# Sparse attention on one core: the weights of two key tiles added by a DMA ahead of one denominator product

## What is computed

```python
logits = jnp.einsum('ehd,ehd->eh', q[rows] * scale, k[cols]) + att_bias
row_max = jax.ops.segment_max(logits, rows, num_segments=n)
p = jnp.exp(logits - row_max[rows])
denom = jax.ops.segment_sum(p, rows, num_segments=n)
att = p / denom[rows]
y = jax.ops.segment_sum(att[:, :, None] * v[cols], rows, num_segments=n)
out = y.reshape(n, H * DK) @ Wo + bo
```

## Time and profile before

| what | us |
|---|---|
| median of 3 runs (1346.62 to 1350.23) | 1347.47 |
| profiled execution, its device time | 1348.99 |
| its span (first to last instruction) | 1347.1 |
| PE busy in the span | 1224.8 |
| DVE busy | 856.7 |
| ACT busy | 419.0 |
| POOL busy | 306.6 |

### The profile page before, as it was taken

How to read it: one execution, slowest core, us unless ns; L and a number is a source line. 1 busy time by engine, 2 the same in 40 slices (tenths; PEclk the granted TensorE clock), 3 DMA queues, 4 the chain that set the end, 5 groups by cost and what they waited for, 6 DMA issues and landing times.

```text
span 1347.1 us, 22146 instructions
## 1 busy us (share of the span) xinstructions
PE 1224.8 (91%) x8447; PEld 549.8 (41%) x8448; DVE 856.7 (64%) x1174; ACT 419.0 (31%) x564; POOL 306.6 (23%) x220
## 2 busy tenths in 40 slices
PE   6888888697879899999999999989999999999996
PEld 2233333232334233344445443444332555555552
DVE  7476666142334555553378873647999787978876
ACT  2445555321123112212311002125541443433331
POOL 2011110000000133354555655555470000000000
PEclk9999999899899999999999999999999899999998
DMA  8688896899681677845122212113222665545552
GB/s 321 238 277 267 270 293 184 310 381 387 206 304 49 230 262 258 286 106 173 2 33 48 48 12 54 2 7 36 31 41 74 227 212 188 186 163 185 174 167 77
DMA packets 65099, 228.02 MB, mean 169 GB/s; under 512 B 31272, under 2 KB 36136, under 8 KB 48790
## 3 DMA queue, kind: packets, MB, share of 16 engines
q1 hardware_dynamic: 35192, 159.02, 34.5%
q0 software_dynamic: 25184, 53.10, 15.7%
q10 hardware_dynamic: 4638, 14.69, 3.1%
HBM read 201.56 MB, written 62.56 MB: 196 GB/s over the span
## 4 chain that ended last, share of the span: by engine, by line
PE 61%; DMA 14%; DVE 10%; issue 10%; ACT 3%; ACTq 1%; DVEq 1%; SPq 0%
PE PS L1657 17%; PE PS L1560 7%; PE PS L1632 7%; PE PS L1902 4%; DMA w_d<-W 4%; DMA R<-in_basis_s 4%; PE PS L1784 4%; PE PS L1889 3%; PE PS L1496 3%; PE PS L1919 3%; DVE R L1119 3%; PE PS L1514 3%; DMA R<-in_attr_t 2%; PE PS L1908 2%; PE PS L1550 2%
## 5 line engine op out<-in xcount | busy, mean ns | idle before, releaser
L735 POOL DMA_INDIRECT bias_d<-R x160 | 268.9, 1680 | 355.9 <-DMA bias_d<-R 231.4
L1657 PE MATMUL PS<-R 128*128 128x512 f16 x1300 | 298.1, 382 | 11.4 <-DMA R<-sup_d 9.8
L1657 PEld LDWEIGHTS PS<-R 128*128 128x128 f16 x1300 | 121.3, 98 | 195.0 <-issue 61.1
L1460 ACT ACTIVATE R<-PS 128x1024 f32<-128x1024 f32 (+1 forms) x100 | 100.4, 1005 | 166.6 <-PE PS L1889 166.6
L1560 PE MATMUL PS<-R,XX 125*128 125x512 f16 (+2 forms) x612 | 129.2, 343 | 24.7 <-DVE R L849 15.0
L1632 PE MATMUL PS<-W,XX 128*128 128x512 f16 x600 | 137.6, 389 | 8.6 <-DVE R L923 7.7
L1119 DVE SCALAR_TENSOR_TENSOR R<-R,W 128x1024 f32<-128x1024 f32 (+1 forms) x68 | 133.0, 1984 | 7.2 <-ACT R L1460 5.9
L1084 DVE CUSTOM_DVE_ANT_0 R<-PS,R 128x1250 f16<-128x1250 f32 x80 | 116.8, 1460 | 5.6 <-PE PS L1836 3.0
L849 DVE TENSOR_SCALAR R<-W,R 125x1250 f16<-125x1250 f16 x160 | 89.5, 605 | 44.4 <-PE PS L1560 40.1
L1902 PE MATMUL PS<-R 128*32 128x256 f32 (+1 forms) x1600 | 105.9, 382 | 5.5 <-DVE R L1119 4.8
L1889 PE MATMUL PS<-R 128*128 128x256 f16 (+3 forms) x800 | 107.3, 277 | 1.7 <-DVE R L1084 1.1
(11 more groups left out here) (215 smaller groups left out, 1395.8 us busy)
## 6 DMA issues: line engine op xcount, KB each, us to landing
bias_d<-bias_d POOLq DMA_DIRECT2D x39, 1280.0 KB, 10.7
R<-in_basis_s SPq DMA_DIRECT2D x48, 1024.0 KB, 10.2
W<-bias_d SPq DMA_DIRECT2D x27, 1024.0 KB, 5.0
R<-bias_d SPq DMA_DIRECT2D x13, 1024.0 KB, 4.9
W<-in_basis_s SPq DMA_DIRECT2D x12, 1024.0 KB, 9.7
R<-key_d SPq DMA_DIRECT2D x20, 500.0 KB, 4.3
R<-R SPq DMA_DIRECT2D x120, 80.0 KB, 6.6
W<-bias_d SPq DMA_DIRECT2D x7, 904.0 KB, 4.6
```

The costliest lines, as they stand in the source:

```text
L735: pool.indirect_dma_start(bias_d, bass.IndirectOffsetOnAxis(ap=idx[:, c:c + 1], axis=0), attr[:, c, :], None, bounds_check=DUMP + GC * P - ...
L1460: S.activation(ER[:, n % 4, :].rearrange("p (h r) -> p h r", h=4)[:, :, 0:w], PS[:, 2 * (n % 2):2 * (n % 2) + 2, :].rearrange("p a (e r) - ...
L1657: ins = T.matmul(mm_out(4 + i % 2, D), lhs, rhs, start=n == 0, stop=n == len(terms) - 1)
```

## The change

In the loop, POOL issues a DMA which adds the 512 KB of one step's weights onto those of another, in SBUF, for two neighbouring key tiles of the same quad and block. `PAIRS` lists these pairs of steps (one, last), 47 of them, sorted by last; from the second block on, last = one + 2. POOL waits until `last` is weighed (`p_made`) and until the values' product has read the slot of `one` (`pv_done`). PE makes one denominator product for the pair (`paired`), two steps behind `last`, in place of two products. Six steps keep their own denominator product (`SINGLE`): two of the first block, and the four of the last pair of key tiles in the last block.

The slots are six instead of four (`ERS`). Exp of step n waits for `pv_done` of step n-6, and further: where n-6 is the first of a pair, for that pair's denominator product (`den_done`), and where it is the second, for the DMA that read it (`pair_added`). DVE reads the denominators at m = 3 instead of 0, inverts at 4, 5, 7, 8, multiplies at 6 and 9, and adds residuals at 13 and 19; PE projects at 11 and 17.

```diff
--- before.py
+++ after.py
@@ -289,7 +289,9 @@
         yT = XT
         BW = 4 * RB
         BR = [w_b[:, 0:2 * BW], w_b[:, 2 * BW:4 * BW], r1f[:, half:half + 2 * BW]]
-        ER = r1f[:, half + 2 * BW:half + 6 * BW].rearrange("p (s n) -> p s n", s=4)
+        ERS = [r1f[:, half + (2 + n) * BW:half + (3 + n) * BW] for n in range(4)]
+        ERS += [r2[:, HEADS * NN + n * BW:HEADS * NN + (n + 1) * BW] for n in range(2)]
+        NE = len(ERS)
         assert 6 * BW <= half
         NB = len(BR)
         Wo = W[:, 2, :, :]
@@ -414,6 +416,8 @@
         e_made = sem("e_made")
         p_made = sem("p_made")
         pv_done = sem("pv_done")
+        summed_up = [sem(f"summed_up{k}") for k in range(4)]
+        den_done = sem("den_done")
         den_read = sem("den_read")
         rden_made = sem("rden_made")
         y_read = sem("y_read")
@@ -497,6 +501,16 @@
 
         ORDER = [(t, q) for q in range(QUADS) for t in range(NB)]
         ORDER += [(t, q) for t in range(NB, NRB * NT) for q in range(QUADS)]
+
+        PAIRS = sorted(((ORDER.index((rb * NT + 2 * p, q)), ORDER.index((rb * NT + 2 * p + 1, q)))
+                        for rb in range(NRB) for p in range(NT // 2) for q in range(QUADS)
+                        if (rb, p, q) != (0, 1, 0) and (rb, p) != (NRB - 1, NT // 2 - 1)), key=lambda pair: pair[1])
+
+        def pair_added(k):
+
+            return summed_up[k % 4], 16 * (k // 4 + 1)
+
+        SINGLE = [n for n in range(STEPS) if not any(n in pair for pair in PAIRS)]
 
         def width(rb):
             return min(RB, NODES - rb * RB)
@@ -735,6 +749,10 @@
                     pool.indirect_dma_start(bias_d, bass.IndirectOffsetOnAxis(ap=idx[:, c:c + 1], axis=0),
                                             attr[:, c, :], None, bounds_check=DUMP + GC * P - 1, oob_is_err=True,
                                             compute_op=ALU.add).then_inc(scattered, 16)
+            for n, last in PAIRS:
+                pool.wait_ge(p_made, last + 1)
+                pool.wait_ge(pv_done, n + 1)
+                pool.dma_start(ERS[n % NE], ERS[last % NE], accum_op=ALU.add).then_inc(pair_added(PAIRS.index((n, last)))[0], 16)
 
         CONST = 12
         SMALL_LOADS = 4 + len(BIASES)
@@ -1115,13 +1133,16 @@
                 dve.wait_ge(e_made, n + 1)
                 dve.wait_ge(bias_rd[t % NB], 16 * (t // NB + 1))
                 w = width(t // NT)
-                p = ER[:, n % 4, :].rearrange("p (h r) -> p h r", h=4)[:, :, 0:w]
+                p = ERS[n % NE].rearrange("p (h r) -> p h r", h=4)[:, :, 0:w]
                 V.scalar_tensor_tensor(p, p, BIG,
                                        BR[t % NB].rearrange("p (r h) -> p h r", h=HEADS)[:, 4 * q:4 * q + 4, 0:w],
                                        ALU.min, ALU.mult).then_inc(p_made, 1)
 
             def denominators(rb):
-                dve.wait_ge(pv_done, QUADS * NT * (rb + 1))
+                if rb < NRB - 1:
+                    dve.wait_ge(den_done, QUADS * NT // 2 * (rb + 1) - 1)
+                else:
+                    dve.wait_ge(pv_done, STEPS)
                 if rb:
                     dve.wait_ge(y_made, QUADS * rb)
                 w = width(rb)
@@ -1162,15 +1183,15 @@
             for n in range(STEPS):
                 rb, m = divmod(n, QUADS * NT)
                 weigh(n)
-                if rb and m == 0:
+                if rb and m == 3:
                     denominators(rb - 1)
-                if rb and m in (1, 2, 4, 5):
+                if rb and m in (4, 5, 7, 8):
                     half = (m - 1) % 3
-                    inverted(rb - 1, m // 4, half)
-                if rb and m in (3, 6):
-                    divided(rb - 1, m // 6)
-                if rb and m in (9, 15):
-                    residual(2 * (rb - 1) + (m == 15))
+                    inverted(rb - 1, m // 7, half)
+                if rb and m in (6, 9):
+                    divided(rb - 1, m // 9)
+                if rb and m in (13, 19):
+                    residual(2 * (rb - 1) + (m == 19))
             denominators(NRB - 1)
             for q in range(QUADS):
                 for half in range(2):
@@ -1454,10 +1475,15 @@
             for n in range(STEPS):
                 rb, m = divmod(n, QUADS * NT)
                 act.wait_ge(st_done, n + 1)
-                if n >= 4:
-                    act.wait_ge(pv_done, n - 3)
+                if n >= NE:
+                    act.wait_ge(pv_done, n - NE + 1)
+                    for k, (one, last) in enumerate(PAIRS):
+                        if one == n - NE:
+                            act.wait_ge(den_done, k + 1)
+                        if last == n - NE:
+                            act.wait_ge(*pair_added(k))
                 w = width(rb)
-                S.activation(ER[:, n % 4, :].rearrange("p (h r) -> p h r", h=4)[:, :, 0:w],
+                S.activation(ERS[n % NE].rearrange("p (h r) -> p h r", h=4)[:, :, 0:w],
                              PS[:, 2 * (n % 2):2 * (n % 2) + 2, :].rearrange("p a (e r) -> p (a e) r", e=2)[:, :, 0:w],
                              ACT.Exp, scale=DK ** -0.5).then_inc(e_made, 1)
                 if rb and m in (0, 1):
@@ -1899,16 +1925,30 @@
                     pe.wait_ge(y_read, QUADS * (rb - 1) + q + 1)
                 for e in range(2):
                     for i in range(4):
-                        T.matmul(PS[32 * i:32 * i + 32, 4 + q, e * RB:e * RB + w],
-                                 VA[:, j, 4 * q + i, 32 * e:32 * e + 32], ER[:, n % 4, i * RB:i * RB + w],
+                        ins = T.matmul(PS[32 * i:32 * i + 32, 4 + q, e * RB:e * RB + w],
+                                 VA[:, j, 4 * q + i, 32 * e:32 * e + 32], ERS[n % NE][:, i * RB:i * RB + w],
                                  start=j == 0 and e == 0, stop=j == NT - 1, skip_group_check=True)
-                if j == 0 and rb:
-                    pe.wait_ge(den_read, rb)
+                if n in SINGLE:
+                    ins = denominator(n, n == SINGLE[0], j == NT - 1)
+                ins.then_inc(pv_done, 1)
+
+            def denominator(n, first, last):
+
+                t, q = ORDER[n]
+                w = width(t // NT)
                 for i in range(4):
                     ins = T.matmul(PS[32 * i:32 * i + 32, 6, q * RB:q * RB + w], ones[:, 0:32],
-                                   ER[:, n % 4, i * RB:i * RB + w],
-                                   start=j == 0 and q == 0, stop=j == NT - 1, skip_group_check=True)
-                ins.then_inc(pv_done, 1)
+                                   ERS[n % NE][:, i * RB:i * RB + w], start=first, stop=last, skip_group_check=True)
+                return ins
+
+            def paired(k):
+
+                n, last = PAIRS[k]
+                (t, q), rb = ORDER[n], ORDER[n][0] // NT
+                pe.wait_ge(*pair_added(k))
+                if t % NT == 0 and rb:
+                    pe.wait_ge(den_read, rb)
+                denominator(n, rb > 0 and t % NT == 0 and q == 0, t % NT == NT - 2).then_inc(den_done, 1)
 
             def projected(i):
 
@@ -1932,11 +1972,14 @@
                 rb, m = divmod(n, QUADS * NT)
                 if n + 2 < STEPS:
                     scores(n + 2)
+                for k, (one, last) in enumerate(PAIRS):
+                    if last == n - 2:
+                        paired(k)
                 weighted(n)
                 if n == QUADS * NT:
                     pe.wait_ge(wo_in, 16)
-                if rb and m in (8, 14):
-                    projected(2 * (rb - 1) + (m == 14))
+                if rb and m in (11, 17):
+                    projected(2 * (rb - 1) + (m == 17))
             for i in range(2 * (NRB - 1), NT):
                 projected(i)
 
```

## The result

The changed kernel takes 1415.45 us (median of 4 runs, 1413.55 to 1420.98) beside 1347.05 for the kernel before in the same comparison: the ratio is 1.051, with an interval of 1.048 to 1.055. It is slower. The prediction was 1350, with a range of 1324 to 1380; the time lies 35 us above its upper end.

What follows compares the result with a forecast made beforehand. PE was taken as the bound, DVE next; its gain is eaten by the wait for adds. Middle blocks three times +0.4, projections' delays included, first +0.6, last +0.8: +2.6 in all, median 1350.1 us, range 1324 to 1380.

Steps and rivals of the forecast that it cites:

- What bounds the kernel now: Loop's middle blocks: PE sets the pace at 2.43 us a step, 58.0 us a block; DVE is next with 47.6.
- What is removed: 47 denominator products, 25.9 us of PE's queue; 6 to 7 us a block if nothing else waited; moved steps cost nothing.
- The add alone: One accumulating DMA without other traffic: 0.7 + 0.5 + 2.5 transfer + 0.8, so L = 4.5 us.
- L: Time from the end of `weigh(last)` to the add's landing; even with the old pace at 5.8 us, without projections.
- The adds aren't alone: Two adds and two 1 MB loads meet in four steps: L is 5.3 to 5.5 for A, 6.8 for B.
- A: First of two adds in four steps, one step before B; forecast to land with L = 5.3 to 5.5 us.
- B: Second add, whose `weigh` end also releases a load; forecast to land near 9.2 us, L = 6.8.
- the first rival: Short add: transfer of 1.23 us, PE stays the bound, middle blocks 52 us, 1320 in all; chance 0.17.
- Load and B share the rest: After A, both share the DMA engines: 5.6 us of work left at 3.1, ending at 8.7 to 9.0.
- The chain: Loop from add through product, exp and `weigh` to the next add: L + 3.9 us for four steps, 10.7 over B.
- the second: Rival: an add takes 3.7 us, the DMA queues become the bound, cycle 12.9 us, middle blocks 64.5, 1382; chance 0.22.
- The third rival: PE's clock falls to 1.2 GHz for a tenth of the loop after waits: 25 us more, 1375; chance 0.06.

Runs made afterwards that it cites:

- quad 0 alone: Changed kernel with only quad 0's pairs (19 adds, no load released with them), product four steps behind, denominators read as before the change: 1342.36 us, ratio 0.996.
- quad 1 alone: Changed kernel with only quad 1's pairs (19 adds, a load released with each), product four steps behind, denominators read as before the change: 1349.99 us, ratio 1.001.

## Why the prediction was wrong

**What bounds the kernel now**: right. PE's queue was the bound, DVE next.

**What is removed**: the 25.9 us of products are right, what they are worth is not. I had 6 to 7 us a block if nothing else waited; the kernel without adds gives 3.5, and 12 in all, of which the moved projections and residuals alone give 5. Two terms were wrong here. DVE paces the part of the block with the reciprocals once PE's step is 2.16 us. And "`inverted`, `divided` and `residual` only move ... I cost that at nothing" hid a gain of 5 us, at which DVE's wait at the residual would have hinted: 34.9 us in 8 waits in the window of the earlier trace rows, more than any other wait there but ACT's. Both are small beside the 65 us missed.

**The add alone**: nearly right. I had 2.5 us of transfer and L = 4.5; it is 2.7 us, and L = 4.8 with the least landing of 4.5, 5.4 with the median of 5.1. The Trainium skill ("Collectives: The Full Stack", section "The bandwidth ceiling: the fold count and why AG ≠ RS ≠ AR") puts the halved rate of a reduce step down to the second read of its add. The runs come near this: 1 MB written by adds takes 5.4 us of the DMA engines, 1.75 times the load's 3.1. The estimate of 3.2 us for the whole DMA by the Trainium skill ("DMA: Bandwidth & Descriptors", section "Anatomy of one DMA — SWDGE (gpsimd) path") is below every landing of 512 KB here, the least being 4.5; its formula has no term for an add. I also held the load of the earlier trace rows against this formula, though SP issued it and the formula is for a DMA from POOL.

**"The adds aren't alone"**: this is the step that failed and carried the miss. L was forecast as 5.3 to 5.5 for A and 6.8 for B, and is 6.6 and 9.6. A load's transfer was taken as 2.5 us, from the peak of 426 GB/s. But the earlier trace rows had the number: the DMA engines were busy 0.54 of 57.97 us with ten loads, 3.1 us each, and 3.3 beside adds. The 2.8 us by which L was missed split as follows. The sum itself was short: 3.1 + 5.6 is 8.7, and with the 0.8 to the waiting engine B lands at 9.5, not 9.2, which is L = 7.1 (in the first rival B lands at 7.6, not 7.1). With 3.3 and 2.7 for the transfers the same working gives 3.1 + 6.8 + 0.8 = 10.7, L = 8.3. For the 1.3 left there are two candidates: the ends of an add alone, 0.7 us longer than my 2.0 (5.4 less 2.7), and the load that was released a step ahead of A and still moves then, which I had left out. That they add up to it is an argument, not measured apart. "Load and B share the rest" was also wrong as a picture: the load goes first and the add behind it. For B this changes nothing, as its landing is the end of both transfers either way.

**The chain**: the mechanism is right, L + 3.9 for four steps (14.2 in the turn above, with L = 9.8 and 0.4 for the clock). With half loads B's L was 7.0, and the blocks were 59.8, 62.1 and 57.4 where the forecast had 58.4 for 6.8. What was too low is its price: I had 18 us for 1 us of L, the runs show some 20; the first block alone lost 22 us where I had 0.6. 2.8 x 20 = 56 of the 65 us missed.

**The rivals**: the second, that the DMA engines become the bound, came nearest, 1382 with a cycle of 12.9. I had put its condition on the add alone, from 3 us on. The condition is on the sum of the four transfers, above 11 us, and it was met by the loads: 2 x 3.3 + 2 x 2.7 = 12.0. That alone would be 60 us a block. To it come some 2 us in every turn in which nothing moves, where I had 0.5; these 14 us for four steps are 70 for a block. With half adds or half loads the sum was under PE's 9.7 us and time was lost all the same, so the chain and not the sum alone decides. The third rival, PE's clock, was rightly seen as to the mechanism: PE's groups L1915, L1928 and L1940 together took some 21 us more for the same products than in the kernel before. How much of it is in the time I can't separate; in the turn shown it was 0.4 us of 14.2. With the adds or the loads made small the clock was 0.975, as in the kernel before, so it fell with the waits and not with the new order of the products. The short add (the first rival) didn't occur.

**The range**: its upper end took half of the second rival in, with a cycle put together from the same 2.5 us for a load. One number that was too small thus stood in the forecast and in the rival, and the range was too narrow for both. The chances inside the forecast don't follow from its range either: spread evenly over 1332 to 1368, 0.55 has 0.18 below 1343.5 and 0.25 above 1351.5, not 0.23 and 0.20.

Open is why the DMA engines serve a load ahead of an add that is issued 0.26 us behind it. The traffic shows that they do, not by what rule.

## What to carry to other kernels

Before you give a transfer to the DMA engines inside a loop, add up the engine time of all transfers of a turn, each from its mean share in a block (share x us / count), never from the peak rate. If the sum comes near the turn's length, count for the one that something waits for also the transfers that go ahead of it: here the load that the same `weigh` released. Look also for an engine that waits for another's result at the head of its queue (here DVE at the residual): to move this and the projection, with a step more between them, gave 5 us, and nineteen adds with their removed products gave nothing on top.

## What the runs showed of the hardware

- An accumulating DMA of 512 KB within SBUF took 2.7 to 3.0 us of the 16 DMA engines (2.7 after the change, 3.0 with quad 0 alone) and landed 4.5 us after POOL's start at the least; POOL itself was held 0.87 us by its issue, against 0.52 for the plain ones of the earlier trace rows.
- Issued 0.26 us behind a load of 1 MB, an add of 32 KB landed in 4.8 us, without a load in 2.8; one of 512 KB in 9.2 against 5.1. In the 4 us in which the load moved 0.78 MB (1171.2:1175.2 of the kernel with quad 1 alone) no packet of the add moved.
- A load of 1 MB cost 3.1 us of the 16 engines in the kernel before, at a peak of 426 GB/s, and 3.3 beside adds.
- POOL's sum of two tiles of 128x1024 in fp32 took 3.85 us, and DVE's operation on other tiles of that size took 0.5 to 0.6 us more in that kernel (2.45 and 2.60 for 1.98 on the mean).
- After a wait of 3.7 us PE's product took 1.08 us in place of 0.64, at a granted clock of 0.50.
